# Fetching the Toeplitz tables of a state-space mixer as lower triangles, in three transfers by row range

## The chip, the cores and the metric

The kernel runs on one core of one Trainium2 chip (trn2). The metric is the device time of one execution in microseconds (us); lower is better. Engines are called TensorE (PE, its weight loads PEld), VectorE (DVE), ScalarE (ACT), GpSimd (POOL) and SyncE (SP). SP does no arithmetic here: it issues DMAs from its queue.

## What is computed

One block of a sequence model on 8 sequences of 512 tokens with 128 features, all in float32:

```
xz = einsum('bld,ed->bel', x, W_in); u, z = split(xz)          # 256 channels each
u = silu(causal depthwise conv(u, 4 taps) + conv_b)
k = 2 Re( sum_n Ct[h,n] exp(dtA[h,n] t) )                       # (256, 512)
y = irfft(rfft(u, 2L) * rfft(k, 2L))[..., :L]                    # causal convolution of length 512
y = (y + u * D) * silu(z)
x = layernorm(x + einsum('bhl,dh->bld', y, W_out))
e = argmax(x @ gate_w.T + gate_b + expert_bias)                  # top 1 of 8 experts
x = layernorm(x + relu(x @ w1[e] + b1[e]) @ w2[e] + b2[e])
```

## The kernel before

The causal convolution is done without a transform. A sequence is cut into 4 chunks of 128 tokens. Within a chunk the convolution of a channel is a product with a 128 x 128 Toeplitz matrix; between chunks it goes through 8 states of each channel.

The stages follow one another: (1) up to about 82 us the input projection with the convolution taps folded in (`project`, L1155 and L1158), beside which the tables of exponentials and sines are built on VectorE and ScalarE; (2) from 85 to 141 us the mixer, a loop over 32 groups of 8 channels; (3) the output projection, the first norm and the choice of experts (L1256 to L1290), with rows scattered by expert (L529); (4) 39 blocks of 128 rows through the experts (L1311 to L1332).

The table. The first 128 values of each channel's kernel are summed (L1180), written in reverse order into `Kx` (L939), with 128 zeros behind them, and stored to DRAM as `kernel_rows`, 256 floats a channel (L385 to L387). The access pattern `toeplitz` (L79) reads that row with a step of one element from partition to partition: partition p of channel h holds row[p + u] for u = 0 to 127. So where p + u is 128 or more it reads a zero. A group's table is 128 partitions x 8 channels x 128 columns, 512 KB.

The ring. `Tring` (a view of `TR`) has 8 slots. `load_toeplitz(r, k)` (L389 to L395) issues the table of group r * 8 + k from SP's queue. The first 8 are issued as soon as the kernel rows are stored; then come the output weights (L400), and in a loop over r the other 24, each after the products of the group 8 before it (`s_tm`). Each slot has its own semaphore `s_t[k]`, which one table raises by 16. Before the mixer parts of `TR` hold other things: `Sel` in slot 0, `empties` in slot 1, `Kx` in slot 4, and on partition 0 alone a row of convolution weights in slot 5 and a row of ones in slot 6.

The order in the mixer is written out by hand. For each group TensorE runs `mix`: 24 small matmuls that sum the states (L1200), then, after the wait for `s_t[k]` at L1203, 16 matmuls in records, 8 in the code, with the table (L1207). Then it runs `finish` of the group before: two transposes of the product (L1217) and one product with the output table (L1221). The first 8 groups are unrolled; the other 24 run in a loop of three turns with 8 groups in its body. POOL scales the state table of a group (`group_tables`, L476), ScalarE applies silu to a group's input (L638) and copies the product (L648), VectorE scales the states (L953) and applies the gate (L966). POOL's work at the start is a row of memsets and selects (L446 to L467), which ends with the identity matrix; then it waits for the output table (L481).

```
                sp.dma_start(Tring[:, k, :, :], toeplitz[:, bass.ds(group * GH, GH), :]).then_inc(s_t[k], 16)
```

Of the kernel before, what the change touches and what calls it, by code (L numbers as in the profile page):

```python
# [14 lines left out]
P = 128  # L15
BATCH, SEQ, DM = 8, 512, 128
CHAN, STATES, TAPS = 256, 8, 4
EXPERTS, DFF = 8, 512
TOKENS = BATCH * SEQ
CHUNK = P  # L20
# [3 lines left out]
GH = 8  # L24
# [4 lines left out]
SCOLS = LAGS * BATCH  # L29
KLEN = CHUNK + 1  # L30
KROW = 2 * CHUNK
BLOCKS = TILES + EXPERTS - 1
REGION = TOKENS + P
EMPTY_ROW = EXPERTS // 2 * REGION
# [16 lines left out]

T_SLOTS = 8
LAG_ORDER = (3, 1, 2)
X_BANKS, Z_BANKS = (0, 1, 4, 5), (2, 3, 6, 7)
A_BATCH = 4
XPAD = TAPS - 1
# [5 lines left out]
def wait_past(engine, semaphore, count):  # L62

    if not isinstance(count, int) or count > 0:
        engine.wait_ge(semaphore, count)
# [9 lines left out]
def build(nc, hidden_t, w_in_t, conv_w, conv_b, states, d_skip, w_out, gate_w_t,  # L75
          gate_b, expert_bias, w1, b1, w2, b2, out):
    kext = nc.dram_tensor("kernel_rows", [CHAN, KROW], F32).ap()
    rows_dram = nc.dram_tensor("decay_and_turns", [2, P * GROUPS], F32).ap()
    toeplitz = bass.AP(kext.tensor, 0, [[1, P], [KROW, CHAN], [1, CHUNK]])  # L79
    slots_dram = nc.dram_tensor("dispatched_rows", [SLOT_ROWS, ROW], F32).ap()  # L80
    out_rows = out.rearrange("b l d -> (b l) d")

# [1 line left out]
    with ctx:  # L84
        def sb(name, shape, dt=F32):
            return ctx.enter_context(nc.sbuf_tensor(name, shape, dt))

        def sem(name):
            return ctx.enter_context(nc.semaphore(name))
# [20 lines left out]
        Tring = TR[:, :].rearrange("p (s h u) -> p s h u", s=T_SLOTS, h=GH)  # L110
# [24 lines left out]
        mask8 = sb("mask8", [P, GH])  # L135
        Kx = TR[:, 4096:4096 + 2 * KROW].rearrange("p (j c) -> p j c", j=2)
        dskip = sb("dskip", [P, 2])
# [23 lines left out]
        first = EN[:, 3744:3776].rearrange("p (k e) -> p k e", k=4)  # L161
# [3 lines left out]
        def late(at, shape, dt=F32):  # L165
            view = CR[:, LATE + 768 + at:LATE + 768 + at + shape]
            return view if dt == F32 else view.bitcast(dt)
# [5 lines left out]
        total = late(72, EXPERTS)  # L173
        brow = EN[:, 2200:2200 + BLOCKS + 1]
        row_steps = EN[:, 2240:2240 + (BLOCKS + 1) * KINDS].rearrange("p (b e) -> p b e", e=KINDS)
        back = EN[:, 2608:2608 + KINDS]
        base = EN[:, 2624:2624 + KINDS]
        bexpf = late(136, BLOCKS + 1)
        bexp = late(176, BLOCKS + 1, I32)
        cnt = late(400, 5 * KINDS).rearrange("p (i e) -> p i e", e=KINDS)  # L180
        erow = EN[:, 2192:2200]
        bstart = late(264, BLOCKS + 1)
        first_row = late(304, BLOCKS + 1, I32)
        OH = EN[:, 0:64].rearrange("p (s k e) -> p s k e", s=2, e=EXPERTS)
# [39 lines left out]
        s_cb = sem("conv_bias_loaded")  # L224
        s_wx = sem("conv_weights_ready")
        s_const = sem("constants_ready")
        s_pstep = sem("pool_step")
        s_vstep = sem("vector_step")
        s_exp1 = sem("rates_ready")
# [32 lines left out]
        s_t = [sem(f"toeplitz_loaded{k}") for k in range(T_SLOTS)]  # L262
# [89 lines left out]
        def _(sp):  # L352
# [36 lines left out]
            def load_toeplitz(r, k):  # L389
                group = r * T_SLOTS + k  # L390
                if not isinstance(r, int):

                    sp.wait_ge(s_tm, group - (T_SLOTS - 1))

                sp.dma_start(Tring[:, k, :, :], toeplitz[:, bass.ds(group * GH, GH), :]).then_inc(s_t[k], 16)  # L395

            for k in range(T_SLOTS):
                load_toeplitz(0, k)
            sp.wait_ge(s_xb, PAIRS)
            sp.dma_start(w_out_d, w_out).then_inc(s_wo, 16)  # L400
            with sp.Fori(1, GROUPS // T_SLOTS) as r:
                for k in range(T_SLOTS):
                    load_toeplitz(r, k)
# [36 lines left out]
        def _(pool):  # L440
# [26 lines left out]
            nc.gpsimd.affine_select(out=ident[:, :], in_=ident[:, :], compare_op=ALU.is_equal, fill=0.0, base=0,  # L467
                                    pattern=[[-1, P]], channel_multiplier=1).then_inc(s_const, 1)


            def group_tables(r, k):
                g = r * 2 + k
                wait_apart(pool, s_s, g - 1)
                one = bass.ds(g, 1)
                falls = decay.rearrange("p m (s n g) -> p (m s) n g", s=STRIPS, g=GROUPS)[:, :, :, one].rearrange("p m n g -> p m (n g)")
                nc.gpsimd.tensor_tensor(  # L476
                    BC[:, k, 0:LAGS, :].rearrange("p m (s r n) -> p (m s) r n", s=STRIPS, r=2),
                    Btab[:, :, :, :, :, one].rearrange("p m s r n g -> p (m s) r (n g)"),
                    falls.unsqueeze(2).to_broadcast([P, LAGS * STRIPS, 2, PAIR * STATES]), ALU.mult).then_inc(s_bc, 1)
# [69 lines left out]
        def _(act):  # L549
# [30 lines left out]
            def state_sines(i):  # L580

                for q, scale, bias in ((1, TWO_PI, 0.0), (0, -TWO_PI, quarter[:, :])):
                    rows = Btab[:, LAG_ORDER[i] - 1, :, q, :, :].rearrange("p s n g -> p s (n g)")
                    act.wait_ge(s_bt, i * 2 + 2)
# [169 lines left out]
        def _(dve):  # L754
# [44 lines left out]
            def state_turns(i, step):  # L799
                lag = tau[:, LAG_ORDER[i] - 1:LAG_ORDER[i]]  # L800
                for half in range(2):
                    row = turns_row[:, half * 1024:half * 1024 + 1024].rearrange("p (s q) -> p s q", s=2)
                    part = Btab[:, LAG_ORDER[i] - 1, half * 2:half * 2 + 2, :, :, :].rearrange("p s r n g -> p s r (n g)")
                    cosine, sine = part[:, :, 0, :], part[:, :, 1, :]
                    if step:
                        dve.wait_ge(s_bw, i * 6 + ((step - 1) * 2 + half + 1))
                    if step == 0:
                        ts(cosine, row, lag, MAGIC, ALU.mult, ALU.add).then_inc(s_bw, 1)
                    elif step == 1:
                        ts(cosine, cosine, MAGIC, None, ALU.subtract).then_inc(s_bw, 1)  # L810
                    elif step == 2:
                        stt(sine, row, lag, cosine, ALU.mult, ALU.subtract).then_inc(s_bw, 1)
                    else:
                        stt(cosine, sine, -1.0, sine, ALU.mult, ALU.max).then_inc(s_bt, 1)
# [322 lines left out]
        def _(pe):  # L1137
# [38 lines left out]
            for q in range(4):  # L1176
                for strip in range(4):
                    for half in range(2):
                        g = half * 16 + strip * 4 + q
                        last = mm(bank[4 + half][strip * 32:strip * 32 + 32, 0:CHUNK], Sel[:, g, :], Ctab[:, g, 0:CHUNK],  # L1180
                                  start=(q == 0), stop=(q == 3))
# [6 lines left out]
            def mix(r, k):  # L1188
                g = r * T_SLOTS + k
                s, yt = bank[6 + k % 2], bank[k % 2]  # L1190
                xg = XG[:, k % 2, :, :]
                out_s = s[:, 0:PAIR * SCOLS].rearrange("p (h c) -> p h c", h=PAIR)
                pe.wait_ge(s_xg, g + 1)
                pe.wait_ge(s_bc, g + 1)
                wait_past(pe, s_v, g - 1)
                for lag in range(LAGS):
                    cols = SCOLS - lag * BATCH
                    for strip in range(STRIPS):
                        at = slice(strip * STRIP, (strip + 1) * STRIP)
                        last = mm(out_s[at, :, lag * BATCH:], BC[:, k % 2, lag, at],  # L1200
                                  xg[:, strip * PAIR:(strip + 1) * PAIR, 0:cols], start=(lag == 0), stop=(lag == LAGS - 1))
                last.then_inc(s_s, 1)
                pe.wait_ge(s_t[k], (r + 1) * 16)  # L1203
                wait_past(pe, s_yt, g - 1)
                for h in range(GH):
                    at, part = h // 4 * P, h % 4 * TILES
                    last = mm(yt[part:part + TILES, at:at + P], xg[:, h, :], Tring[:, k, h, :], start=True, stop=True)  # L1207
                last.then_inc(s_tm, 1)
# [16 lines left out]
            pe.wait_ge(s_kx, 2)  # L1225
            pe.wait_ge(s_const, 3)
            mix(0, 0)
            for k in range(1, T_SLOTS):
                mix(0, k)
                finish(0, k - 1)  # L1230
            with pe.Fori(1, GROUPS // T_SLOTS) as r:
                for k in range(T_SLOTS):
                    mix(r, k)
                    finish(r, k - 1)
# [6 lines left out]
            for j in range(2):  # L1241
                last = mm(bank[3][:, j * (DM + EXPERTS):(j + 1) * (DM + EXPERTS)], w_out_d[:, j * P:j * P + P], centre[:, :],
                          start=True, stop=True)
# [153 lines left out]
```

## Time and profile before

| | us |
|---|---|
| median of 3 runs | 288.48 |
| lowest, highest | 286.81, 288.93 |
| the profiled execution | 288.91 |
| its span, first to last instruction | 287.2 |
| mean granted TensorE clock | 0.944 |

Times in rows are microseconds from the start of the span, durations of single instructions in nanoseconds where a row says so. "xN" is a count of instructions. In square brackets of a timeline stands how long the engine was idle before the instruction, and what ended that: a line of another engine, a DMA, or "issue", which means that the profile shows nothing it waited for. "SPq" is SP's queue: the time is that of issuing a DMA. The granted clock is a share of full speed. The DMA share is the busy time of the 16 DMA engines over 16 times the stretch; packets overlap, so it can be above 1. The queue named "instruction" carries program code.

### The profile page before, as it was taken

To read this page: it belongs to the slowest core of one execution; us is meant where nothing else is said; L and a number is where in the kernel's file an instruction comes from. 1 tells how busy PE (TensorE), PEld (TensorE's weight loads), DVE (VectorE), ACT (ScalarE), POOL (GpSimd) and SP (SyncE) were. 2 spreads that over 40 slices of the span, in tenths; PEclk is the share of its full clock that TensorE was granted. 3 is DMA by queue.
4 is the path that set the end of the run, shared out by engine and by line. 5 is a ranking of instruction groups with operands and counts; after the bars stand their busy time and mean duration, and the time that the engine had idled before them with its cause. 6 is when DMAs were issued, how large, how long until landed. Compare 5 with 4: busy or idle time off the path is not lost.

```text
span 287.2 us, 8709 instructions
## 1 busy us (share of the span) xinstructions
PE 245.9 (86%) x2801; PEld 217.6 (76%) x2801; DVE 171.1 (60%) x532; ACT 188.1 (65%) x522; POOL 125.7 (44%) x143
## 2 busy tenths in 40 slices
PE   4799999999957987999979999610999999999980
PEld 1688888888845655677769999500899999999970
DVE  2889985999354342455524565780066666676772
ACT  5879999846986664778746565200477777777740
POOL 5000000400049575999401777774004555544555
PEclk9999999999999797999999999955599999999996
DMA  6748977200399999998092321125367777677510
GB/s 215 213 111 343 346 291 279 118 0 0 118 289 332 282 316 275 248 317 229 3 346 96 96 86 57 51 60 188 97 191 212 213 206 215 195 203 208 173 37 5
DMA packets 54243, 52.12 MB, mean 181 GB/s; under 512 B 4399, under 2 KB 42801, under 8 KB 54082
## 3 DMA queue, kind: packets, MB, share of 16 engines
q1 hardware_dynamic: 50930, 45.60, 52.8%
q0 software_dynamic: 2272, 4.27, 4.3%
q10 hardware_dynamic: 1008, 1.84, 1.9%
q8 instruction: 18, 0.29, 0.4%
q14 instruction: 15, 0.12, 0.2%
HBM read 38.14 MB, written 14.00 MB: 182 GB/s over the span
## 4 chain that ended last, share of the span: by engine, by line
PE 82%; POOL 5%; issue 5%; DMA 2%; DVE 2%; ACT 2%; SPq 0%; DVEq 0%; ACTq 0%; POOLq 0%
PE banks L1155 20%; PE banks L1321 13%; PE banks L1332 11%; PE banks L1207 6%; PE banks L1158 5%; PE banks L1273 5%; POOL dispatched_rows L529 4%; PE banks L1217 4%; PE banks L1200 4%; PE banks L1221 4%; PE banks L1256 2%; PE banks L1271 2%; PE banks L1311 2%; PE banks L1290 1%; PE banks L1165 1%
## 5 line engine op out<-in xcount | busy, mean ns | idle before, releaser
L1155 PE MATMUL banks<-Wx,XT 128*128 128x256 f32 x256 | 62.4, 388 | 1.4 <-DVE Wx L785 1.4
L544 POOL DMA_INDIRECT out<-X x39 | 38.3, 982 | 49.3 <-DVE X L1111 40.5
L737 ACT ACTIVATE Z<-banks,BR 128x128 f32<-128x128 f32 x156 | 44.7, 367 | 20.4 <-PE banks L1321 20.2
L1155 PEld LDWEIGHTS banks<-Wx,XT 128*128 128x128 f32 x256 | 49.6, 195 | 10.1 <-DVE Wx L785 3.0
L476 POOL TENSOR_TENSOR Wx<-BR,RE 128x384 f32 (+1 forms) x32 | 47.9, 1524 | 8.8 <-PE banks L1200 8.8
L1321 PE MATMUL banks<-Z 128*128 128x128 f32 x312 | 43.4, 285 | 0.0
L529 POOL DMA_INDIRECT dispatched_rows<-TR,CR x32 | 31.3, 977 | 23.1 <-issue 22.1
L1332 PE MATMUL banks<-BR,Z 128*128 x312 | 40.9, 275 | 0.0
L1321 PEld LDWEIGHTS banks<-Z 128*128 128x128 f32 x312 | 40.0, 201 | 0.1
L1332 PEld LDWEIGHTS banks<-BR,Z 128*128 128x128 f32 x312 | 37.8, 192 | 0.0
L966 DVE TENSOR_TENSOR X<-banks,Z 128x256 f32 (+1 forms) x32 | 13.6, 425 | 26.9 <-PE banks L1221 26.8
L1094 DVE TENSOR_TENSOR X<-banks,X 128x128 f32<-128x128 f32 x39 | 11.4, 291 | 22.8 <-PE banks L1332 21.5
L721 ACT ACTIVATE Z<-banks 128x128 f32<-128x128 f32 x39 | 11.4, 291 | 19.4 <-PE banks L1311 19.4
L1207 PE MATMUL banks<-TR,RE 128*32 128x128 f32 x512 | 22.1, 289 | 1.9 <-issue 1.9
L1311 PE MATMUL banks<-ident,X 128*128 128x128 f32 x39 | 11.3, 290 | 14.2 <-DMA X<-dispatched_rows 14.2
L793 DVE TENSOR_TENSOR X<-banks,cbias 128x512 f32<-128x512 f32 x16 | 16.8, 1068 | 8.6 <-PE banks L1158 8.6
L648 ACT ACTIVATE RE<-banks 128x256 f32<-128x256 f32 x32 | 12.3, 383 | 14.5 <-PE banks L1207 13.5
L1200 PEld LDWEIGHTS banks<-RE,Wx 128*32 128x32 f32 x768 | 10.6, 114 | 14.4 <-issue 13.6
L482 POOL MEMSET RE<- 128x128 f32 x1 | 0.2, 204 | 47.0 <-DVE CR L901 47.0
L1273 PE MATMUL banks<-Wx,RE 128*128 128x136 f32 x128 | 20.1, 279 | 0.0
L1158 PE MATMUL banks<-Win,XT 128*128 128x256 f32 x64 | 19.0, 379 | 0.0
L1221 PE MATMUL banks<-Win,Wx 128*128 128x192 f32 x64 | 16.6, 340 | 1.9 <-issue 1.9
(195 smaller groups left out, 463.0 us busy)
## 6 DMA issues: line engine op xcount, KB each, us to landing
TR<-kernel_rows SPq DMA_DIRECT2D x32, 512.0 KB, 6.4
Z<-w SPq DMA_DIRECT2D x35, 256.0 KB, 2.9
dispatched_rows<-TR SPq DMA_DIRECT2D x3, 2310.0 KB, 8.8
X<-dispatched_rows SPq DMA_DIRECT2D x39, 66.0 KB, 2.7
XT<-hidden_t SPq DMA_DIRECT2D x10, 256.0 KB, 3.3
RE<-decay_and_turns SPq DMA_DIRECT2D x2, 1024.0 KB, 7.3
BR<-w SPq DMA_DIRECT2D x1, 2048.0 KB, 8.1
dispatched_rows<-TR SPq DMA_DIRECT2D x1, 1848.0 KB, 7.9
```

Of the source, the lines that this page charges most:

```text
L476: nc.gpsimd.tensor_tensor(BC[:, k, 0:LAGS, :].rearrange("p m (s r n) -> p (m s) r n", s=STRIPS, r=2), Btab[:, :, :, :, :, one].rearrange(" ...
L529: pool.indirect_dma_start(slots_dram, bass.IndirectOffsetOnAxis(pos[:, batch, k:k + 1], 0), X1[:, batch, k, :], None).then_inc(s_sc[batch] ...
L544: pool.indirect_dma_start(out_rows, bass.IndirectOffsetOnAxis(XS[:, n % ROWS_RING, TOKEN_COL:TOKEN_COL + 1].bitcast(U32), 0), F[:, slot, : ...
L737: last = nc.scalar.activation(HT[:, slot, c * P:c * P + P], bank[n % 4][:, c * P:c * P + P], ACT.Relu, bias=B1[:, bass.ds(experts[n % 4] * ...
L1155: mm(bank[X_BANKS[k]][:, j * CHAN:(j + 1) * CHAN], XT[:, slot, at:at + CHUNK], Wx[:, tap, :], start=(tap == 0), stop=(tap == TAPS - 1))
L1158: last = mm(bank[Z_BANKS[k]][:, j * CHAN:(j + 1) * CHAN], XT[:, slot, at:at + CHUNK], Win[:, CHAN:], start=True, stop=True)
L1200: last = mm(out_s[at, :, lag * BATCH:], BC[:, k % 2, lag, at], xg[:, strip * PAIR:(strip + 1) * PAIR, 0:cols], start=(lag == 0), stop=(lag ...
L1207: last = mm(yt[part:part + TILES, at:at + P], xg[:, h, :], Tring[:, k, h, :], start=True, stop=True)
L1221: mm(y[:, 0:GH * TILES].rearrange("p (h t) -> p h t", h=GH)[:, :, BATCH:], BC[:, slot, LAGS, :], V[:, slot, :, :], start=False, stop=True) ...
L1273: last = mm(projected(slot, k), GT[:, slot, k, j * P:j * P + P], Wo[:, j, :], start=False, stop=(j == 1))
L1321: last = mm(bank[n % 4][:, c * P:c * P + P], WS[:, stage, c * P:c * P + P], XsT[:, n % DEEP, :], start=True, stop=True)
L1332: last = mm(bank[6 + n % 2][:, 0:P], HT[:, n % DEEP, c * P:c * P + P], W2[:, e, c * DM:(c + 1) * DM].rearrange("p e d -> p (e d)"), start= ...
```

## The change

The table is fetched in three transfers by partition range. `T_PARTS` gives for each the first partition, the one behind the last, and the columns: partitions 0 to 31 all 128 columns, 32 to 63 the first 96, 64 to 127 the first 64. What is left out is zero in every table. In slots 2, 3, 5, 6 and 7 GpSimd writes those zeros once, right after the identity matrix, and SP waits for the four memsets before the first table. In slots 0, 1 and 4, which hold other things until then, the first table is fetched at full width, also in three transfers, and brings its own zeros. Each table raises its semaphore by 48.

```
+T_PARTS = ((0, 32, CHUNK), (32, 64, CHUNK - 32), (64, P, CHUNK - 64))
+T_ZEROED = (2, 3, 5, 6, 7)
...
-    toeplitz = bass.AP(kext.tensor, 0, [[1, P], [KROW, CHAN], [1, CHUNK]])
+    toeplitz = [bass.AP(kext.tensor, low, [[1, high - low], [KROW, CHAN], [1, CHUNK]]) for low, high, _ in T_PARTS]
...
-                sp.dma_start(Tring[:, k, :, :], toeplitz[:, bass.ds(group * GH, GH), :]).then_inc(s_t[k], 16)
-
+                for (low, high, width), part in zip(T_PARTS, toeplitz):
+                    cols = CHUNK if isinstance(r, int) and k not in T_ZEROED else width
+                    sp.dma_start(Tring[low:high, k, :, 0:cols], part[:, bass.ds(group * GH, GH), 0:cols])                      .then_inc(s_t[k], 16)
+
+            sp.wait_ge(s_tz, 4)
             for k in range(T_SLOTS):
                 load_toeplitz(0, k)
...
+            pool.wait_ge(s_const, 3)
+            for i, (low, high, cols) in enumerate(T_PARTS[1:]):
+                for j, (first, last) in enumerate(((2, 4), (5, T_SLOTS))):
+                    nc.gpsimd.memset(Tring[low:high, first:last, :, cols:], 0.0).then_inc(s_tz, 1)
+                    pool.wait_ge(s_tz, i * 2 + (j + 1))
...
-                pe.wait_ge(s_t[k], (r + 1) * 16)
+                pe.wait_ge(s_t[k], (r + 1) * 48)
```

## Rows read from the trace of the kernel before

**Rows 1.** The page: span, and busy time, share and instructions of each engine.

```profile
span 287.2 us, 8709 instructions
PE 245.9 (86%) x2801; PEld 217.6 (76%) x2801; DVE 171.1 (60%) x532; ACT 188.1 (65%) x522; POOL 125.7 (44%) x143
```

**Rows 2.** Windows: stretch, length; busy (instructions) PE PEld DVE ACT POOL; clock, DMA, GB/s.

```profile
92.00:98.00 6.00, 4.82 (x96) 3.29 (x95) 1.66 (x5) 2.51 (x7) 3.41 (x4) 0.72 1.06 295
98.00:104.00 6.00, 5.58 (x150) 3.95 (x146) 2.90 (x8) 4.71 (x14) 5.65 (x4) 1.00 1.08 307
104.00:110.00 6.00, 4.31 (x121) 3.14 (x122) 2.03 (x5) 3.19 (x10) 4.48 (x3) 1.00 1.06 300
110.00:116.00 6.00, 4.84 (x97) 3.31 (x100) 1.69 (x4) 2.48 (x7) 2.68 (x3) 0.72 1.02 278
...
122.00:128.00 6.00, 6.00 (x179) 4.31 (x178) 3.29 (x9) 4.88 (x15) 6.00 (x5) 1.00 1.13 314
```

**Rows 3.** Timeline of PE in the mixer: start, length, line, out<-in, count, idle before.

```profile
85.60 0.28 PE L1207 MATMUL banks<-TR,RE 128*32 128x128 f32 x1
...
93.18 0.43 PE L1207 MATMUL banks<-TR,RE 128*32 128x128 f32 x8 [1.74 <-issue]
...
104.93 0.31 PE L1200 MATMUL banks<-RE,Wx 128*32 128x32 f32 x14 [1.34 <-issue]
...
108.91 0.33 PE L1221 MATMUL banks<-Win,Wx 128*128 128x192 f32 x1
111.16 0.32 PE L1221 MATMUL banks<-Win,Wx 128*128 128x192 f32 x1 [1.92 <-issue]
...
125.35 0.40 PE L1200 MATMUL banks<-RE,Wx 128*32 128x48 f32 x24
...
126.83 0.40 PE L1200 MATMUL banks<-RE,Wx 128*32 128x48 f32 x24
...
140.47 0.62 PE L1207 MATMUL banks<-TR,RE 128*32 128x128 f32 x16
```

**Rows 4.** Issues of line 395 on SP: whole run, landing, then in 99.8 to 103.6.

```profile
L395 SPq DMA_DIRECT2D TR<-kernel_rows x32: 372/756/2382, 75.8 to 129.4; - x32
DMA to landing us min/median/max: 3.8/6.4/8.1
...
L395 SPq DMA_DIRECT2D TR<-kernel_rows x3: 1202/1713/1729, 99.8 to 103.6; - x3
```

**Rows 5.** DMA queues in 86.9:90.6, 90.6:90.8, 104.9:108.7, 108.7:108.9, 114.4:114.6, 116:141, in that order.

```profile
q1 hardware_dynamic: 2432, 1.23, 110.9%
...
q8 instruction: 1, 0.02, 27.5%
...
q1 hardware_dynamic: 2171, 1.09, 103.2%
...
q8 instruction: 1, 0.02, 28.8%
...
q8 instruction: 1, 0.02, 30.0%
...
q1 hardware_dynamic: 10603, 5.34, 78.4%
```

In the first, third and last of these stretches q1 is the only queue. The columns are packets, MB, and their time as a share of 16 engines.

**Rows 6.** DMA queues over the whole span: the one that ScalarE issues to.

```profile
q10 hardware_dynamic: 1008, 1.84, 1.9%
```

**Rows 7.** Timeline of POOL and DVE at the start, and POOL's next work.

```profile
3.07 0.95 POOL L460 MEMSET TR<- 128x1024 f32 x1
...
4.78 0.29 POOL L467 TENSOR_SCALAR_AFFINE_SELECT ident<-ident 128x128 f32<-128x128 f32 x1
...
7.66 1.28 DVE L785 TENSOR_TENSOR Wx<-Win,banks 128x512 f32<-128x512 f32 x2 [2.07 <-PE banks L1165]
...
52.07 0.20 POOL L482 MEMSET RE<- 128x128 f32 x1 [47.00 <-DVE CR L901]
```

More of the change, by code:

```diff
@@ L226, in build @@
         s_const = sem("constants_ready")
+        s_tz = sem("toeplitz_zeros_ready")
         s_pstep = sem("pool_step")
```

## The prediction

> **What bounds the kernel now.** Read the page first. The span is 287.2 us and TensorE is busy 86% of it [rows 1], so a change to transfers can pay only where TensorE stands still. The tables are fetched from 75.8 to about 135 us, so the second view is the windows of the mixer stage [rows 2]. In an undisturbed window of 6 us (122 to 128) TensorE runs 179 matmuls at clock 1.00. Between 92 and 116 us, 24 us, it runs 96 + 150 + 121 + 97 = 464, which would take 464 / 179 x 6 = 15.6 us. So 8.4 us are lost there, and two windows stand at clock 0.72. The DMA share in all of them is over 1.00, in 122 to 128 as well.
>
> The tempting reading is that TensorE waits for a table. The timeline of PE says otherwise [rows 3]. An undisturbed group starts 1.48 us after the one before (125.35 to 126.83). The gaps before 93.18 (1.74 us), 104.93 (1.34) and 111.16 us (1.92), together 5.0, are put down to "issue", no semaphore, and two of the three lie inside a run of matmuls of one line: 93.18 inside the eight products of a group and 104.93 inside the state sums, which read no table. Nor is the ring of tables late. The first table is issued at 75.83 and lands at best 3.8 us later [rows 4]; its first matmul is at 85.60. The last one is issued at 129.4 and even with the longest landing of 8.1 us it is there at 137.5, while its first matmul is at 140.47.
>
> What is short in those gaps is instructions. DMA windows show it [rows 5]. In the 3.7 us from 86.9 the table queue alone holds 110.9% of the 16 engines and no instruction block moves; one begins inside 90.6 to 90.8, and TensorE resumes at 93.18. After the second gap none moves from 104.9 to 108.7; one begins inside 108.7 to 108.9, and TensorE resumes at 111.16. From the third gap's end to 114.4 the same: one at 114.4 to 114.6. From 116 to 141, when the loop over groups repeats code that is already there, no block moves and TensorE has no such gap, with the table queue at 78.4% over that stretch. So each block begins 3.2 to 3.8 us after TensorE resumed, which is about two tables of queued traffic, and needs about 2.4 us more to be usable. That is 5.6 to 6.2 us. I read a block as lasting TensorE about 4.2 us at full speed, from the 4.0 to 4.3 us between 104.93 and the last matmul before the stop, which starts at 108.91 and takes 0.33. The wait in front of it, not its own length, makes the gap; it may be under 4.2 - 2.4 = 1.8 us, about one table, before a gap appears. The Trainium skill ("Runtime: NRT & Kernel Launch", Instruction fetch mechanics) says that instructions are refilled in 16 KiB blocks by a DMA queue while the current ones run. The trace agrees in size: 0.02 MB in each such window. The sum below does not need it.
>
> **The change, part by part.**
> *Bytes.* A table is 128 x 8 packets of 512 B. After, from the second turn of the ring on, it is 256 of 512, 256 of 384 and 512 of 256 B: 68.75% of the bytes, as many packets. In the first turn slots 0, 1 and 4 keep full width. What a packet costs by size is seen from two rows. In 86.9 to 90.6, 1.109 x 16 x 3.7 us / 2432 = 27.0 ns per packet, nearly all 512 B. Queue q10 has 1008 packets of 1825 B in 1.9% x 16 x 287.2 us = 86.6 ns [rows 6]. The line through both is 3.8 ns + 0.0454 ns per B: 384 B take 21.2 and 256 B 15.4 ns, and a table costs (256 x 27.0 + 256 x 21.2 + 512 x 15.4) / (1024 x 27.0) = 0.73 of now. Ends: 0.69 if bytes alone count, 1.00 if a packet costs the same whatever its size, and above 1 if a transfer over 32 or 64 partitions is slower per byte, which no row here shows. Now a table takes 0.524 MB / 1.23 MB x 3.7 = 1.58 us at best and 1.83 us at the mean of 104.9 to 108.7 [rows 5]. I take 0.76, for some loss in three short pieces: 1.2 to 1.4 us, under the 1.48 us that TensorE needs.
>
> *Issues.* 96 in place of 32. Free ones took 372 ns [rows 4]; with some 0.08 us of register work for each and 0.28 us of waiting between tables I get 3 x 0.45 + 0.25 = 1.6 us per table. That is SP's pace, near TensorE's 1.48, and below what an issue costs now when the queue is full (median 1713 ns in 99.8 to 103.6). Behind the longer issue on SP stand only the next tables and, after the eighth, the output weights, which nothing reads before the last group is done. 24 tables x (1.6 - 1.48) = 2.9 us of delay, against a lead of at least 140.5 - 137.5 = 3.0 us: cost 0, bounded by 0 and 3 us. Its good side: SP can no longer hold two tables queued in front of an instruction block, once the first eight are through.
>
> *Zeroing.* Four memsets of 512, 768, 1024 and 1536 elements, 3840 in all. 1024 took 0.95 us [rows 7], so 3.6 us, right behind the last select of POOL at 4.78. POOL then idles until 52.07, so it hides; SP's new wait is met by 10 us, 65 us before the first issue. If VectorE were held meanwhile it would cost up to 3.6 us; but it stands idle for 2.07 us before 7.66 [rows 7], waiting for TensorE. Cost taken 0, bounds 0 and 3.6. TensorE's wait for 48 instead of 16 adds the landing of two more pieces and nothing else, with the slack above.
>
> *What goes.* The first gap stays: at 86.9 us the first eight tables (three of them full) are still queued. From about 92 us tables leave faster than they are asked for, so under one table is queued when the second and third block are wanted. Gone are 1.34 and 1.92 us, and the slow clock behind the third gap: window 110 to 116 ran 97 of 178 matmuls, 2.7 us lost, of which 1.16 are the gap's, so 1.6. Sum 4.9 us. The stages behind start that much earlier, unchanged. 288.9 (the profiled execution) - 4.9 = **284.0 us**; the median shown is 288.5, so by it the gain is 4.5. A difference of 1%, 2.9 us, is about what can be told here.
>
> **Rivals.**
> *B, nothing moves (288.5).* The three pieces cost a table as much as now, ratio 0.95 to 1.15, so the queue in front of the blocks is as long. For it: same number of packets, and no row has a 256 B packet from these tables. The Trainium skill ("SBUF — State Buffer", Door 1: The DMA port swizzle) speaks for it: partitions 0 to 63 reach 8 of 16 ports and 64 to 127 the other 8, and two transfers on the two halves do not add up. By its 218 GB/s for half the ports, 360 KB take 1.65 us, as an estimate. No transfer of this trace covers under 128 partitions at size, so nothing here tests it.
> *C, all three gaps go (280.5).* Ratio 0.69 and a short queue already at 87 us: 288.9 - 8.4. Against it: the first eight tables are issued in a burst.
> *D, tables become the bound (294).* A transfer that covers half the partitions runs at half the rate of now: 1.58 x 2 x 0.6875 = 2.17 us, and a full-width one 3.16. The first table would land at 79.6 + 1.5 = 81.1 us. Behind it, with a full table counted as 1.45 narrow ones, come 2 x 1.45 + 29 = 31.9, and the last must be there at 140.5. It decides from (140.5 - 81.1) / 31.9 = 1.86 us per table on. At 2.17 the end moves by 31.9 x 2.17 - 59.4 = 9.8 us; at 2.02, the middle, by 5.0, and 288.9 + 5.0 = 294; the gaps are then hidden behind that wait. For it: three transfers with partial partition ranges; against: an engine is held 27 ns for a packet of 512 B now, and a third of the bytes goes.
> *E, a cost elsewhere (290.5).* VectorE held by the zeroing, or SP's pace, for 2 us.
>
> **How the numbers follow.** A 0.40, B 0.25, C 0.12, D 0.17, E 0.06. Faster by over 1%: C and 0.34 of A, 0.46. Within 1%: the rest of A, most of B and half of E, 0.34. Slower by over 1%: D and the other half of E, 0.20. Range 280.5 to 292.0: it holds A, B, E, most of C, and the mild part of D. A's own range is 282 to 287.
>
> **What would show it.** Right: only one or two "issue" gaps of TensorE in 85 to 116 us, window 110 to 116 at clock 1.00 with over 150 matmuls, DMA share well under 1 after 100 us, issues of some 0.4 us, an instruction block beginning under 2 us after the previous one is entered. Wrong: TensorE waiting for a table at the product's line (D), three gaps as long as now at a DMA share over 1 (B), or a packet of 256 B that holds an engine 25 ns or more.

## The result, and the profile after

The change makes the kernel slower: 294.28 us median (293.81 to 296.78, 4 runs) against 288.51 us (286.81 to 288.93, 4 runs), a ratio of 1.023 with a 95% interval of 1.016 to 1.030. Ratios here and below compare the fast executions alone, so a ratio can differ a little from that of the two medians. The forecast was 284.0 us. Its sum went wrong above all in one term, the issues. The time came out where rival D had put it, for another reason than D gave and in part by luck.

From the page of the changed kernel: its span, the queue of the tables, the chain that ended last, and the issues of tables:

```profile
span 292.8 us, 8874 instructions
...
q1 hardware_dynamic: 51954, 40.85, 50.9%
...
PE 66%; POOL 9%; issue 8%; SPq 8%; DMA 3%; DVE 2%; ACT 2%; DVEq 0%; POOLq 0%; ACTq 0%
...
TR<-kernel_rows SPq DMA_DIRECT2D x64, 128.0 KB, 3.3
...
TR<-kernel_rows SPq DMA_DIRECT2D x29, 96.0 KB, 3.0
```

The bytes are gone (q1 moved 45.60 MB before, 40.85 now), but SP's queue, which held 0% of the chain that ended last before, now holds 8%. The windows of the changed kernel, beside [rows 2]:

```profile
86.00:92.00 6.00, 5.37 (x156) 4.37 (x160) 2.70 (x6) 4.46 (x14) 5.03 (x4) 0.72 1.02 228
92.00:98.00 6.00, 6.00 (x192) 4.25 (x178) 3.29 (x9) 4.88 (x15) 6.00 (x5) 1.00 0.79 158
98.00:104.00 6.00, 5.34 (x154) 3.93 (x149) 2.77 (x7) 3.96 (x12) 5.04 (x5) 1.00 0.73 159
...
110.00:116.00 6.00, 5.62 (x173) 3.94 (x172) 3.04 (x8) 4.25 (x13) 5.34 (x5) 1.00 0.79 160
...
122.00:128.00 6.00, 5.31 (x148) 3.73 (x148) 2.55 (x7) 3.40 (x10) 4.44 (x4) 1.00 0.87 189
128.00:134.00 6.00, 4.92 (x140) 3.38 (x132) 2.10 (x6) 3.81 (x11) 4.46 (x4) 1.00 0.94 178
```

The two halves of the stage moved in opposite directions. From 92 to 116 us TensorE is better off: windows that ran 96 and 97 matmuls at clock 0.72 run 192 and 173 at 1.00. One window at 0.72 is there all the same, from 86 to 92 us. After 116 us it is worse off: 148 and 140 where 179 and 178 ran. In the timeline of PE group 16 is reached at 113.88 in place of 118.16 and the last group at 143.90 in place of 140.47. From the first product to group 16 the stage went from 32.6 to 26.9 us, 5.7 gained; from there to the last from 22.3 to 30.0, 7.7 lost.

What TensorE waits for in the mixer of the changed kernel (us in total, times, longest):

```profile
PE banks L1218 <- DMA TR<-kernel_rows: 4.7, 12, 0.9
...
PE banks L1211 <- issue: 0.7, 1, 0.7
PE banks L1232 <- issue: 0.6, 1, 0.6
PE banks L1218 <- issue: 0.4, 1, 0.4
```

The waits for code, which the profile puts down to "issue", are down from 5.0 us [rows 3] to 1.7. New are twelve waits for a table, at the product's line. SP's own timeline, then all its issues of tables, and the row of landings, beside [rows 4]:

```profile
74.63 14.26 SPq L399 DMA_DIRECT2D TR<-kernel_rows  x24
88.94 0.62 SPq L405 DMA_DIRECT2D cbias<-w_out  x1
89.93 51.04 SPq L399 DMA_DIRECT2D TR<-kernel_rows  x72
```

```profile
L399 SPq DMA_DIRECT2D TR<-kernel_rows x96: 316/452/1390, 74.6 to 140.4; - x96
...
DMA to landing us min/median/max: 2.2/3.1/4.6
```

The loop's 72 issues take 51.04 us, 2.13 us per table, with no wait worth naming for a free slot: the slot of the table issued at 133.4 us (group 28) had been free since group 20 was multiplied at 122. SP works without a pause and cannot keep up with a consumer that needs a table each 1.48 us. The last piece is issued by 140.97, and TensorE starts on its table 2.9 us later, at 143.90.

A second loss lies behind the mixer. From the last table's product to the end the span grew from 146.7 to 148.9 us. In the timeline of POOL the first scatter of rows starts late, here the changed kernel:

```profile
162.84 1.20 POOL L540 DMA_INDIRECT dispatched_rows<-TR,CR  x1 [15.93 <-issue]
```

Its positions are ready on VectorE at 159.48, 3.36 us before. In the kernel before the same two times are 156.04 and 157.08, 1.04 us apart. A third piece of the difference, 1.4 us until the mixer starts (first product at 87.00, before at 85.60), can't be put down to the change: in the runs below it lies at 85.72 and 86.89 with the change's code up to there, and between 85.51 and 87.23 with the code of the kernel before.

### The profile page after: what moved, and what is told of

It reads as the page before. It is cut to its first block, busy times and chain, and to the rows that moved or that the text cites. A ratio compares the mean times of both kernels' runs of the same rounds, so it can differ in the third digit from the quotient of the medians.

```text
span 292.8 us, 8874 instructions
## 1 busy us (share of the span) xinstructions
PE 249.0 (85%) x2801; PEld 219.7 (75%) x2801; DVE 171.6 (59%) x532; ACT 188.7 (64%) x522; POOL 129.4 (44%) x147
## 3 DMA queue, kind: packets, MB, share of 16 engines
q1 hardware_dynamic: 51954, 40.85, 50.9%
## 4 chain that ended last, share of the span: by engine, by line
PE 66%; POOL 9%; issue 8%; SPq 8%; DMA 3%; DVE 2%; ACT 2%; DVEq 0%; POOLq 0%; ACTq 0%
PE banks L1166 20%; PE banks L1332 13%; PE banks L1343 11%; POOL dispatched_rows L540 9%; SPq L399 7%; PE banks L1169 5%; PE banks L1218 3%; PE banks L1211 2%; PE banks L1228 2%; PE banks L1284 2%; PE banks L1232 2%; PE banks L1322 2%; PE banks L1176 1%; DMA TR<-kernel_rows 1%; PE banks L1267 1%
## 5 line engine op out<-in xcount | busy, mean ns | idle before, releaser
L1166 PEld LDWEIGHTS banks<-Wx,XT 128*128 128x128 f32 x256 | 50.1, 197 | 10.4 <-DVE Wx L796 3.0
L977 DVE TENSOR_TENSOR X<-banks,Z 128x256 f32 (+1 forms) x32 | 13.6, 425 | 29.2 <-PE banks L1232 29.1
L1218 PEld LDWEIGHTS banks<-TR,RE 128*32 128x32 f32 x512 | 12.9, 113 | 7.0 <-DMA TR<-kernel_rows 6.3
```

The lines of the kernel that those rows point to most:

```text
L1166: mm(bank[X_BANKS[k]][:, j * CHAN:(j + 1) * CHAN], XT[:, slot, at:at + CHUNK], Wx[:, tap, :], start=(tap == 0), stop=(tap == TAPS - 1))
```

## The experiments

Two theories stood at first. S: SP issues three transfers per table too slowly. T: the transfers themselves, each over 32 or 64 partitions, take too long. Ratios are against runs of the kernel before on the same chip.

### SP's loop written out

```
-            with sp.Fori(1, GROUPS // T_SLOTS) as r:
+            for r in range(1, GROUPS // T_SLOTS):
                 for k in range(T_SLOTS):
                     load_toeplitz(r, k)
```

> The change, with SP's loop over the last 24 tables written out, so that no issue needs register work; the transfers are the same 96. Theory S (the pace of SP's issues sets when a table lands; in the changed kernel 24 tables take 51.0 us on SP, 2.13 us each, and the DMA share is only 0.7 to 0.9): a table takes about 1.8 us of SP, the pace of the first eight, 24 take 43 to 45 us, the last lands near 137 us, TensorE waits for no table, and the time is 284 to 288 us. Theory T (the transfers themselves, over 32 and 64 partitions, take about 2 us per table): the waits for tables and the time of the changed kernel stay, 292 to 296 us.

292.24 us, ratio 1.012 (1.006 to 1.018). The same 96 transfers, and by the two ratios about half of the loss is gone, though their intervals just overlap. So what SP does between them seems to matter, as S says. But S had forecast 284 to 288 us and no waits. Its issues in 116.7 to 133.4 us:

```profile
L399 SPq DMA_DIRECT2D TR<-kernel_rows x29: 450/580/622, 116.7 to 133.4; - x29
```

There is no register work left, and the issues themselves became longer: 620, 451 and 580 ns in turn with 40 ns between them, 1.78 us per table, where the loop has 398, 317 and 605 with 0.63 us of other work, 1.95. Before 116 us four issues took 1.5 to 1.7 us. From its first issue to the end of its last SP needed 62.6 us for all 32 tables, in place of 66.3. But in the profiled execution it began 1.4 us later (76.05 against 74.63), and TensorE still waited 4.7 us for tables. The mixer, from its first product to the last, was only 0.6 us shorter there (56.3 against 56.9). S was right about the place and too hopeful about the size.

### Three transfers of almost nothing

```
-                    cols = CHUNK if isinstance(r, int) and k not in T_ZEROED else width
+                    cols = (CHUNK if k not in T_ZEROED else width) if isinstance(r, int) else 16
```

The product with columns 16 to 127 uses old values from the second turn on.

> The change, but in the loop each of the three transfers of a table brings only its first 16 columns (64 B packets; the rest keeps old values, so part of the product is wrong): a sixth of the bytes, the same 72 issues and as many packets. Theory S (SP's issues with their register work set the pace): SP's pace stays at 1.9 to 2.1 us per table, TensorE still waits for tables late in the loop, 291 to 296 us. Theory T (the transfers' own time over partial ranges sets it): the waits for tables go, under 288 us.

This ran on a slower chip, on which the kernel before took 302.76 us: 308.82 us, ratio 1.025 (1.015 to 1.036), the same as the change. This decides between S and T for the change. In 122 to 134 us it has 12 pieces of 16 KB and the share of all 16 engines is about a third:

```profile
q1 hardware_dynamic: 6303, 0.39, 35.4%
...
TR<-kernel_rows SPq DMA_DIRECT2D x12, 16.0 KB, 2.1
```

and its issues in 117.0 to 133.6 are those of the change, 316 to 637 ns with a median of 396 against 398:

```profile
L399 SPq DMA_DIRECT2D TR<-kernel_rows x26: 316/396/637, 117.0 to 133.6; - x26
```

```profile
PE banks L1218 <- DMA TR<-kernel_rows: 4.0, 12, 0.6
```

Twelve waits again, with next to nothing to move. The time of these issues does not hang on their bytes.

### Two halves at full width

```
+                for low in (0, 64):
+                    part = bass.AP(kext.tensor, low, [[1, 64], [KROW, CHAN], [1, CHUNK]])
+                    sp.dma_start(Tring[low:low + 64, k, :, :], part[:, bass.ds(group * GH, GH), :]).then_inc(s_t[k], 16)
```

> The kernel before, with each table in two transfers of 64 partitions, all 128 columns, same bytes. Theory T (half the partitions, half the rate): 3.2 us per table, the tables bind, over 320 us. Half of it by the measured changed kernel (some loss from the range): 2.0 to 2.4 us per table, 295 to 305. Theory S: still bound by the transfers at 1.6 to 1.8 us per table while the queue is full, issues 1.2 to 1.5 us, time 286 to 291 us.

297.97 us, ratio 1.032 (1.022 to 1.041), in the range of "half of it". TensorE waits 3.9 us for tables, in ten places, and 6.5 us for code. So transfers over half the partitions have a cost of their own. In the change it does not set the pace, as the run before shows. DMA queues in 122 to 134 us:

```profile
q1 hardware_dynamic: 6019, 2.99, 124.7%
```

2.99 MB in 12 us, 0.249 MB per us, with the engines at a share of 1.25: 0.524 MB take 2.1 us, where a table in one transfer took 1.58 [rows 5]. The page of the Trainium skill that the prediction named ("SBUF — State Buffer", Door 1: The DMA port swizzle) has 8 of the 16 ports for 64 partitions. By its 218 GB/s this would be 2.4 us, as an estimate. By half of the rate measured here, 0.332 MB per us, it would be 3.2. The loss is there, and smaller than either: 25% of the rate. Both halves were in the queue at once here, so this is not the rate of one half alone.

### Two transfers, with 75% of the bytes

```
-T_PARTS = ((0, 32, CHUNK), (32, 64, CHUNK - 32), (64, P, CHUNK - 64))
+T_PARTS = ((0, 64, CHUNK), (64, P, CHUNK - 64))
```

> Two transfers per table instead of three: partitions 0 to 63 with 128 columns, 64 to 127 with 64, 75% of the bytes; loop as in the change. Theory S: 0.4 + 0.35 us of issue, 0.15 of registers and 0.25 between tables, 1.2 to 1.5 us per table, below TensorE's 1.48; no waits for tables, shorter queue before instruction blocks, 283 to 287 us. Theory T: each half at half the rate of now, 1.58 x 2 x 0.75 = 2.4 us per table, TensorE waits, 300 us or more.

286.64 us, ratio 0.994 (0.991 to 0.998): faster than the kernel before, by little. Both issues take 0.60 us, a table 1.66 us with the rest, more than S's 1.2 to 1.5 and less than T's 2.4. Over all 32 tables, with the long issues beside blocks of code, it is 1.83 us. TensorE's matmuls never wait for a table, but the lead is then just used up: the last issue starts at 133.8, the median landing is 4.2 us, and the last product starts at 138.0.

### One transfer with fewer bytes

```
-                sp.dma_start(Tring[:, k, :, :], toeplitz[:, bass.ds(group * GH, GH), :]).then_inc(s_t[k], 16)
+                cols = CHUNK if isinstance(r, int) else 88
+                sp.dma_start(Tring[:, k, :, 0:cols], toeplitz[:, bass.ds(group * GH, GH), 0:cols]).then_inc(s_t[k], 16)
```

Columns 88 to 127 keep what an earlier table had there.

> The kernel before, with one transfer per table that brings 88 of 128 columns on all partitions from the second turn of the ring on (68.75% of the bytes; the columns left out keep what the table before had there, so part of the product is wrong). Both theories of the tables: no wait for a table. It tests what fewer bytes are worth alone. If instruction blocks wait behind queued tables, as the prediction says: the gaps of TensorE put down to issue shrink from 5.0 to under 2.5 us and the time is 281 to 286 us. If they do not wait for the queue: 287 to 289 us.

286.92 us, ratio 0.993 (0.989 to 0.998). In the mixer TensorE's waits for code are 3.2 us in place of 5.0, between the two branches of the expectation, and the time is just over the first one's 286 us. The worth of the bytes alone is about 2 us (0.6 to 3.3): less than the 4.9 of the forecast.

### A shorter lead, all bytes

```
-                    sp.wait_ge(s_tm, group - (T_SLOTS - 1))
+                    sp.wait_ge(s_tm, group - (T_SLOTS - 4))
```

> The kernel before, unchanged transfers, but a table of the loop is issued only once the group 5 before it is multiplied, not the group 8 before, so fewer tables are queued while TensorE enters new code. If instruction blocks wait behind queued tables: a block begins within 2 us of the one before being entered, gaps put down to issue fall from 5.0 us to under 2, the clock stays at 1.00 after the first, 282 to 286 us. If the gaps have another cause: 288 to 289 us. If the lead is too short: TensorE waits for tables at the product's line and the time is over 289 us.

On the slower chip: 302.24 us, ratio 1.003 (0.999 to 1.008). The waits for code were 3.8 us, not under 2. The profile has the mixer shorter (51.4 us from the first product to the last against 54.9 in the profile of before on another chip), but the time shows nothing of it. The profiled execution, 298.37 us, was the fastest of the twelve. With two transfers per table as well:

> Two transfers per table in the loop, the first eight whole, and each table of the loop issued once the group 5 before it is multiplied. Fewer bytes and a shorter queue together. If blocks of instructions wait mainly behind queued tables: gaps of TensorE put down to issue under 1.5 us in 85 to 116 us, and 1 to 2 us less than the same without the short lead. If most of a block's wait is there without tables too (it was 1.9 to 2.9 us with 64 B packets at a DMA share of 0.34): no more than 0.5 us of difference.

288.29 us, ratio 0.996 (0.992 to 1.000), against 0.989 with the long lead below. 2.8 us of waits for code, and 1.1 us for tables in three places. Both branches of the expectation missed. A shorter lead is no gain.

### The first eight tables whole

```
+                if isinstance(r, int):
+                    whole = bass.AP(kext.tensor, 0, [[1, P], [KROW, CHAN], [1, CHUNK]])
+                    sp.dma_start(Tring[:, k, :, :], whole[:, bass.ds(group * GH, GH), :]).then_inc(s_t[k], 16)
+                    return
```

Two transfers per table in the loop; no memsets, since the whole tables bring the zeros; TensorE waits for r * 32 + 16.

> As the kernel with two transfers per table, but the first eight tables come whole in one transfer each and nothing is zeroed. The first eight then take 13 to 15 us on the DMA engines at full rate instead of about 15 at the rate of half ranges. Theory: the rate of transfers over 64 partitions (0.246 MB per us at best, against 0.32 whole) costs only in the first eight here, since later SP's 1.66 us per table is the slower; so 285 to 287 us, the same as with two transfers throughout or 1 us less.

On the slower chip 299.90 us, ratio 0.991 (0.985 to 0.997). A second time, on a chip like the first:

> The kernel with two transfers per table and the first eight whole, a second time, to narrow its ratio: 0.988 to 0.997, faster than both kernels.

285.72 us, ratio 0.989 (0.983 to 0.995). This is the lowest ratio found: about 3 us below the kernel before and some 9 below the change. The interval overlaps those of the two transfers throughout (0.991 to 0.998) and of the run that follows.

The same with the change's three transfers and SP's loop written out:

> The change's three transfers with both of SP's costs cut: the first eight tables whole in one transfer each, and the loop of issues written out so that no register work is needed. Theory S: SP's pace is 1.78 us per table and some 1 us more at each of four instruction blocks, so about 1.95 on average over the first half and 1.78 after, just at TensorE's need; few waits for tables, 288 to 291 us by the time of the kernel before of 288.5, a ratio of 0.995 to 1.01. If the bytes or the partial ranges set it, the ratio stays at 1.02.

286.24 us, ratio 0.994 (0.991 to 0.998), better than the 0.995 to 1.01 expected. So the triangle in three pieces is not lost in itself. SP's timeline of this kernel, to be read beside that of the change:

```profile
74.27 10.70 SPq L399 DMA_DIRECT2D TR<-kernel_rows  x8
85.01 1.76 SPq L407 DMA_DIRECT2D cbias<-w_out  x1
86.81 46.62 SPq L402 DMA_DIRECT2D TR<-kernel_rows  x72
```

1.94 us per table in the loop are still more than 1.48, but SP enters it 3.1 us sooner than in the change and needs 4.4 us less in it. From the first issue to the end of the last it is 59.2 us, 1.85 us per table. The waits for tables are one, of 0.7 us, at the last group. Against the run with the loop written out alone, the code differs in the eight issues in place of 24 at the start, and in having no memsets. In the profiled executions SP also began 1.8 us sooner (74.27 against 76.05).

### The zeroing alone

The kernel before with GpSimd's four memsets and SP's wait for them:

```
+            pool.wait_ge(s_const, 3)
+            for i, (low, high, cols) in enumerate(((32, 64, CHUNK - 32), (64, P, CHUNK - 64))):
+                for j, (first, last) in enumerate(((2, 4), (5, T_SLOTS))):
+                    nc.gpsimd.memset(Tring[low:high, first:last, :, cols:], 0.0).then_inc(s_tz, 1)
+                    pool.wait_ge(s_tz, i * 2 + (j + 1))
```

> The kernel before with the change's four memsets of GpSimd and SP's wait for them added, and nothing else; each table still comes whole in one transfer. In the three kernels with four memsets the first scatter of rows starts 3.36 us after its positions are ready, in those with two or none 1.04 us. If the added instructions move the end of a block of GpSimd's code in front of that scatter: the same 3.2 to 3.4 us here, 2.3 us more in time, 290 to 291.5 us, a ratio of 1.006 to 1.01. If that wait comes from the tables' transfers: 288 to 289 us, a ratio of 1.00. Nothing is expected of the memsets' own 3.6 us in either case.

290.02 us against 288.62, ratio 1.006 (1.002 to 1.009). The tables come whole here and TensorE waits for none, and yet there is a loss. POOL's timeline:

```profile
5.13 3.75 POOL L475 MEMSET TR<- 32x512 f32 x4
...
157.93 1.20 POOL L536 DMA_INDIRECT dispatched_rows<-TR,CR  x1 [16.09 <-issue]
```

The only transfer in 155.9 to 156.1 us:

```profile
q14 instruction: 1, 0.01, 9.6%
```

The memsets take 3.75 us where nobody waits, and 150 us later the first scatter starts 3.5 us after its positions are ready at 154.42, not 1.04. All four kernels with four memsets that were profiled show this (the change, its loop written out, the 16 columns, and this one). All the others, with two memsets or none, do not: POOL idles 13.6 us there, not 15.9 to 16.1. Among them is the kernel with three transfers, its loop written out and no memsets, so the transfers are not the cause. A wait for more code fits: in each of the four an 8 KB block of instructions on q14 begins 1.3 to 1.5 us after the positions are ready, and the scatter starts 2.0 to 2.2 us after the block (155.94 and 157.93 us here). In all the others the first such block comes after the first scatter (158.93 against 157.08 in the kernel before). The added memsets and waits of GpSimd would move the place at which it must wait for code. That this is the way it works is inferred, since the profile says only "issue". That the added instructions bring it about is shown; memsets and waits were not tried apart.

### The kernel before once more

> The kernel before, unchanged, for a profile on the chip of the other runs of this call: a ratio of 1.00; three gaps of TensorE put down to issue, 4 to 6 us in all, again in 90 to 112 us, and the block of instructions each time beginning 3 to 4 us after the one before is entered.

Ratio 0.997 (0.992 to 1.002), which is how far equal kernels come apart here. Its waits for code in the mixer were more than in the first profile, and more than expected: five, of 7.7 us in all, in place of three of 5.0.

```profile
PE banks L1207 <- issue: 3.5, 2, 2.0
...
PE banks L1200 <- issue: 2.5, 2, 1.3
PE banks L1221 <- issue: 1.7, 1, 1.7
```

For each run, the rate of all transfers in 92 to 116 us (from the windows) and TensorE's waits for code in 84 to 142 us (from the waits):

| tables fetched | GB/s | us |
|---|---|---|
| three of 16 columns | 33 | 1.0 |
| the change | 158 | 1.7 |
| the change, loop written out | 171 | 2.6 |
| three, first eight whole, loop written out | 179 | 3.7 |
| two, short lead | 183 | 2.8 |
| two, first eight whole (slow chip; again) | 206; 207 | 3.8; 3.7 |
| two | 217 | 3.5 |
| one of 88 columns | 217 | 3.2 |
| two halves at full width | 239 | 6.5 |
| before, short lead | 275 | 3.8 |
| before (and with the zeroing; again) | 295 (297; 298) | 5.1 (5.0; 7.7) |

Waits for code are longer with more traffic beside them, though not in strict order. Each row is one execution, and the kernel before alone came out at 5.1 and 7.7 us. So a difference of under 2.6 us between two rows shows nothing by itself, and whether a shorter queue or fewer bytes helps more stays open.

## Why the prediction was wrong

**The step that failed is the term of the issues.** It put SP's pace at 1.6 us per table, "3 x 0.45 + 0.25", and the cost at 0 with 3 us as the worst. Measured were 2.13 us: 398 + 317 + 605 ns of issues and 0.63 us of register work and waits make 1.95, and four issues of 0.8 to 1.4 us between 96 and 111 us, each beside a 16 KB block of instructions, bring the mean up. The row it rested on, 372 ns, was that of an issue with nothing right before it. An issue straight behind another took about 620 ns where the one before it covered 64 partitions, and 451 and 580 ns (for 32 and for 64 partitions) where that covered 32, as the first eight tables and the run with the loop written out show. The trace of the kernel before had the price as well. Its first three issues stand in series while hardly anything is queued, and only the first of them is free:

```profile
L395 SPq DMA_DIRECT2D TR<-kernel_rows x3: 380/583/777, 75.8 to 76.9; - x3
```

The three-sample row of 1713 ns that the prediction quoted for a full queue was read as the queue's fault alone; that issues in series also have a price of their own was not bounded from above.

**The lead was counted once, at its end.** 24 x (1.6 - 1.48) was set against 3 us. At 2.13 it is 24 x 0.65 = 15.6 us. In the change the table of group 8 is issued at 89.93 for a product at 100.37, and that of the last group at 139.23 for a product at 143.90. So the lead shrank from 10.4 to 4.7 us and took 5.8 us of it. The rest is time by which TensorE fell behind 1.48 us per group, waiting for tables and for code.

**D had the right point, its price in part by luck, and another mechanism.** It named 1.86 us per table as the point from which tables decide, and 294 us. D counted all 32 tables, so the paces to compare are those from SP's first issue to the end of its last, over 32. They are 1.83 us with two transfers (no wait of a matmul), 1.85 with three, the first eight whole and the loop written out (one wait, 0.7 us), 1.96 with the loop written out alone (4.7 us in all), and 2.07 in the change (4.7 us). So the point was right to about 0.1 us. The price was not quite: D moved the end of the mixer by 5.0 us, and it moved by 3.4, of which 1.4 was there when the mixer began. The other 2.2 us came from GpSimd's late scatter, which D did not have. And the pace was SP's, not that of half ranges: with 64 B packets nothing changed. D's own mechanism exists, at 25% less rate for halves, not 50%; it is what the kernel with two full halves pays.

**A's mechanism had an effect, of open size.** Waits for code fell from 5.0 to 1.7 us, and the stage to group 16 was 5.7 us shorter, more than the 4.9 forecast. The other two profiles with whole tables in a full queue (the kernel before once more, and with the zeroing) took 32.2 and 30.3 us to group 16, so against them it was 5.3 and 3.4 us. The clock's part of the forecast, 1.6 us, is not shown to be the change's doing. The change has a slow window of its own at 86 to 92 us, and the kernel before once more ran 92 to 116 us at clock 1.00, with more waits for code than in the first profile. The picture of "the wait in front of it, not its own length" did not come true either: 1.0 us of waits stayed at a DMA share of 0.33, and 3.8 with a short lead. Bytes alone, in one transfer, were worth 2 us. Three signs that the prediction named for being right were there (173 matmuls at clock 1.00 in 110 to 116 us, a DMA share under 1 after 100 us, issues near 0.4 us), and D's sign beside them, later in the loop.

**Bytes.** The prediction took 0.76 of a table's present engine time and a cost per packet that falls with its size. In the run of 64 B packets one held an engine 0.354 x 16 x 12 us / 6303 = 10.8 ns, against 27.0 for 512 B, so small packets are cheaper, as the line had it (3.8 + 2.9 = 6.7 there, too low by 4). But the 0.76 did not come out. The table queue in the kernel before (122 to 128 us), in the change (122 to 134) and with 88 columns in one transfer (122 to 134):

```profile
q1 hardware_dynamic: 3741, 1.88, 112.6%
...
q1 hardware_dynamic: 6537, 2.20, 90.5%
...
q1 hardware_dynamic: 5726, 1.98, 69.8%
```

A packet held an engine 28.9, 26.6 and 23.4 ns. With as many packets per table, the change costs 0.92 of the engine time of before (0.98 by the 27.0 ns that the prediction started from), where the same bytes in one transfer cost 0.81. By the packet records of 92 to 134 us the 256 B packets took the change 19.2 ns on average. The 512 B ones took 38.5, against 29.5 in whole tables and 41.5 in the two full halves. So pieces over part of the partitions gave back most of what the bytes saved. That is near rival B's 0.95 to 1.15. It did not bind in the change, where SP was slower still. At the 1.6 us per table of the forecast the share would have been 26.6 x 1024 / 16 / 1600 = 1.06, as an estimate, and the queue not short.

**Zeroing.** Hidden as forecast: four memsets in 3.75 us (3.6 forecast). VectorE was held for a moment, as E feared: an operation that begins with the first memset at 5.14 us takes 0.56 us in all four kernels with four memsets, 0.99 with two, and 0.20 in those without. The first memset takes 0.52 us with four and 0.95 with two, so the operation ends with it. VectorE had to wait for TensorE after it anyway. The cost of the zeroing came from elsewhere, 1.6 us by its own run (0.6 to 2.5), which was on no list; E had 2 us for other reasons.

**B and C.** B's unchanged queue and C's early short queue did not occur: the DMA share was 1.02 in 86 to 92 us and 0.71 to 0.79 in 92 to 116, and the gaps did not all go. The lower share comes from engine time at 0.92 and, more than that, from SP's pace: its loop took 41.2 us for 24 tables before and 51.0 now.

## What to carry to other kernels

Before a transfer is split, write down the pace of the queue that issues it: the time of an issue that has another right before it, taken from a row where issues stand in series and the engines are not full, plus the register work of a loop, times the number of pieces. Compare that with what the consumer needs per step, not only the bytes; here two pieces fitted into 1.86 us and three in a loop did not, and one issue fewer was worth more than another 6% of the bytes. Take the first, unhurried fetches whole, and let them bring the zeros. And do not book a gap or a slow clock of one profile as a gain before a second profile of the same kernel shows it.

## What the runs showed of the hardware

- SP's issues in series cost 0.45 to 0.62 us, by the number of packets in a transfer and in the one before it (256 or 512), with 64 to 128 columns alike. In the loop, with register work between them, 16 columns made no difference either (median 396 against 398 ns).
- While a 16 KB block of instructions moved in the mixer (0.9 to 1.6 us on one engine), one issue of SP took 0.6 to 1.7 us. In the change and in its copy with 64 B packets none was longer than 0.65 us at any other time in the loop.
- Two alternating transfers over halves of the partitions ran at 0.249 MB per us against 0.33 for one over all, at 512 B packets.
- A VectorE operation of 0.20 us that began with a GpSimd memset at 5.14 us took 0.56 us beside a memset of 0.52 us and 0.99 us beside one of 0.95 us.
- With four memsets of GpSimd at 5 us its first scatter, at 158 to 163 us, started 2.3 us or more later after its positions were ready, in four kernels. Added instructions can cost at a place that has nothing to do with them.
- TensorE waited 1.0 us for code at 33 GB/s and 5.0 to 7.7 us at 295 to 298 GB/s, with a TensorE program that differs only in a wait's value.
